# Fused token, attention and int8 layer: the split global term in one 128-row tile

## The reference

```
h   = einsum('bhid,oi,od->bho', x, weighted_sum, weight)      # x: 4 x 512 x 256 x 4
h   = concat(h, txt)                                          # 4 x (512 + 77) x 256
n   = layernorm(h)
hid = relu(n @ gate_w1 + b1);  gate = sigmoid(hid @ gate_w2 + b2)
U, V = n @ U_w, n @ V_w;       S = cumsum(V, axis=1)
glob = gate * U * S                                           # 32 numbers a row
h   = h + conv3(n) + glob @ out_w + out_b                     # out_w: 32 x 256
h   = h + int8_matmul(layernorm(h), rhs)
```

## Time and profile before

| | |
|---|---|
| median of 3 runs | 103.8 us (103.67 to 104.01) |
| profiled execution, first to last instruction | 102.7 us |
| busy: PE, DVE, ACT, POOL | 92.3, 82.5, 76.1, 70.1 us |
| mean granted clock of TensorE | 0.996 |
| chain that ended last: ACT, POOL, PE, DVE, DMA, issue | 23, 19, 16, 13, 11, 10% |

### The profile page before, as it was taken

One profiled execution on the slowest core, in us unless ns is written; L12 is line 12 of the kernel. 1 busy time (PEld: TensorE's weight loads), 2 busy tenths in 40 slices (PEclk: granted clock), 3 DMA queues, 4 the chain that ended last, 5 costly groups with the idle time before them and its releaser, 6 DMA issues.

```text
span 102.7 us, 2135 instructions
## 1 busy us (share of the span) xinstructions
PE 92.3 (90%) x686; PEld 83.8 (82%) x686; DVE 82.5 (80%) x224; ACT 76.1 (74%) x150; POOL 70.1 (68%) x133
## 2 busy tenths in 40 slices
PE   5999994999997999978989989999999788998870
PEld 5988894999696999968979969998897667987650
DVE  3377694489979988996999999899978988998731
ACT  1328646989996999938889987967698999927510
POOL 2000056979458709998997859998998959899940
PEclk9999999999999999999999999999999999999998
DMA  3999992679899999199993896788000230002513
GB/s 71 290 286 377 253 307 99 175 255 324 145 204 206 263 284 203 24 179 317 249 332 136 134 198 179 126 209 169 13 31 0 105 133 3 6 0 97 191 50 132
DMA packets 8137, 17.35 MB, mean 169 GB/s; under 512 B 855, under 2 KB 4799, under 8 KB 8127
## 3 DMA queue, kind: packets, MB, share of 16 engines
q0 software_dynamic: 2880, 10.49, 43.5%
q1 hardware_dynamic: 4815, 6.47, 19.9%
q10 hardware_dynamic: 432, 0.27, 0.9%
HBM read 14.81 MB, written 2.41 MB: 168 GB/s over the span
## 4 chain that ended last, share of the span: by engine, by line
ACT 23%; POOL 19%; PE 16%; DVE 13%; DMA 11%; issue 10%; SPq 4%; POOLq 0%; ACTq 0%
DMA x_sb<-x_dram 11%; POOL rstd L400 7%; ACT xn L619 4%; ACT x_low L523 4%; POOL rstd L399 4%; POOL x_high L425 4%; SPq L350 3%; DVE stats L694 3%; PE h_ps L1003 3%; ACT convT L573 2%; POOL shift L448 2%; ACT xc L629 2%; DVE amax L809 2%; ACT tmp L531 2%; ACT glob L603 2%
## 5 line engine op out<-in xcount | busy, mean ns | idle before, releaser
L908 PE MATMUL h_ps<-w_high,x_high 128*128 128x256 f32 x112 | 33.8, 302 | 0.1
L912 PE MATMUL h_ps<-w_high,x_low 128*128 128x256 f32 x112 | 31.3, 280 | 0.0
L910 PE MATMUL h_ps<-w_low,x_high 128*128 128x256 f32 x112 | 31.3, 279 | 0.0
L908 PEld LDWEIGHTS h_ps<-w_high,x_high 128*128 128x128 f32 x112 | 21.1, 188 | 1.0 <-issue 0.8
L910 PEld LDWEIGHTS h_ps<-w_low,x_high 128*128 128x128 f32 x112 | 21.1, 189 | 0.2
L912 PEld LDWEIGHTS h_ps<-w_high,x_low 128*128 128x128 f32 x112 | 21.1, 188 | 0.0
L399 POOL TENSOR_SCALAR rstd<-mv 128x2 f32<-128x2 f32 (+2 forms) x21 | 8.6, 410 | 17.4 <-DVE mv L697 16.7
L400 POOL TENSOR_TENSOR rstd<-rstd,exponent 128x2 f32<-128x2 f32 (+2 forms) x21 | 16.8, 798 | 1.8
L694 DVE BATCH_NORM_STATS2 stats<-h_ps 128x6 f32<-128x256 f32 (+1 forms) x36 | 13.8, 420 | 2.9 <-PE h_ps L912 1.6
L619 ACT ACTIVATE xn<-h_ps,shift,rstd 128x256 f32<-128x256 f32 x16 | 8.1, 559 | 6.3 <-POOL shift L448 6.3
L781 DVE SCALAR_TENSOR_TENSOR convT<-xnT,par_sb,convT 128x255 f32<-128x255 f32 (+1 forms) x24 | 12.2, 550 | 0.5 <-ACT convT L573 0.3
(11 more groups left out here) (109 smaller groups left out, 205.0 us busy)
## 6 DMA issues: line engine op xcount, KB each, us to landing
x_high<-x_dram POOLq DMA_DIRECT2D x10, 512.0 KB, 6.4
x_low<-x_dram POOLq DMA_DIRECT2D x10, 512.0 KB, 6.1
x_sb<-x_dram SPq DMA_DIRECT2D x4, 512.0 KB, 9.0
out_dram<-fin SPq DMA_DIRECT2D x8, 256.0 KB
x_sb<-x_dram SPq DMA_DIRECT2D x3, 256.0 KB, 4.3
par_sb<-par_dram SPq DMA_DIRECT2D x1, 325.0 KB, 8.4
txt_sb<-txt_dram SPq DMA_DIRECT2D x1, 308.0 KB
out_dram<-fin SPq DMA_DIRECT2D x4, 77.0 KB
```

The costliest lines, as they stand in the source:

```text
L908: nc.tensor.matmul(h_of(g)[:, t, :], x_high[:, g % RING, kc, at], w_high[:, kc, :], start=(kc == 0 and t == 0), stop=False, skip_group_che ...
L910: nc.tensor.matmul(h_of(g)[:, t, :], x_high[:, g % RING, kc, at], w_low[:, kc, :], start=False, stop=False, skip_group_check=True)
L912: last = nc.tensor.matmul(h_of(g)[:, t, :], x_low[:, g % RING, kc, at], w_high[:, kc, :], start=False, stop=(kc == KC - 1), skip_group_che ...
```

## The change

The tiles `glob3` and `outw3` go. A tile `parts` of 128 rows and 333 columns takes their place: rows 0 to 63 hold the high parts of `glob` as it lies (half 0, half 1), rows 64 to 127 the low parts. ACT makes the high parts of a batch in one copy of 64 rows by 333 columns, DVE the low parts in one subtraction of the same size. Both are at the place that the first half's had. The copy waits for both of POOL's multiplications, and `mix` for the whole batch's parts.

The output weights are laid out with zeros for each half: `out_w` is 128 rows by 2 x 256 columns, in which a half has the weights in its own two blocks of 32 rows (of the high and of the low parts) and zeros elsewhere. They are rounded once (`outw_high`, 128 x 512) and their low part is `outw_low` (128 x 512). `mix` is two products for a tile, `parts` by `outw_high` and `parts` by `outw_low`. (The term low by low, which was left out before, is now in the sum.) The parameters' DMA grows from 650 to 906 columns.

```diff
-    high=(24, 25, 46, 48, 69, 70, 89, 90),
-    low=(19, 20, 36, 38, 54, 57, 69, 72),
+    high=(-1, 24, -1, 46, -1, 69, -1, 89),
+    low=(-1, 19, -1, 36, -1, 54, -1, 69),
...
-    PAR = C_OUTW + D
+    PAR = C_OUTW + HALVES * D
...
-        glob3 = sb("glob3", [3 * R, 2, L], F32R)
-        outw3 = sb("outw3", [3 * R, D], F32R)
+        parts = sb("parts", [2 * HALVES * R, 2, PAIR + T], F32R)
+        outw_high = sb("outw_high", [P, HALVES, D], F32R)
+        outw_low = sb("outw_low", [P, HALVES, D], F32R)
...
-                for n in (0, 1):
-                    nc.scalar.activation(outw3[n * R:(n + 1) * R, :], outw, ACT.Copy).then_inc(outw_high, 1)
+                nc.scalar.activation(outw_high[:, :, :], outw, ACT.Copy).then_inc(outw_rounded, 1)
...
-                    b, half = divmod(g, HALVES)
-                    lo, hi = GLOB_RANGES[half]
-                    act.wait_ge(glob_ready, 2 * b + half + 1)
+                    b = g // HALVES
+                    act.wait_ge(glob_ready, 2 * (b + 1))
                     if b >= 2:
                         act.wait_ge(mix_done, ITEMS_PER_B * (b - 1))
-                    for n in (half, 2):
-                        nc.scalar.activation(glob3[n * R:(n + 1) * R, b % 2, lo:hi],
-                                             glob[half * R:(half + 1) * R, b % 2, 0:hi - lo],
-                                             ACT.Copy).then_inc(glob_high, 1)
+                    nc.scalar.activation(parts[0:HALVES * R, b % 2, :], glob[:, b % 2, :],
+                                         ACT.Copy).then_inc(glob_high, 1)
...
-                nc.vector.tensor_tensor(outw3[2 * R:3 * R, :], outw, outw3[0:R, :].bitcast(F32), ALU.subtract)
+                nc.vector.tensor_tensor(outw_low[:, :, :], outw, outw_high[:, :, :].bitcast(F32),
+                                        ALU.subtract).then_inc(outw_split, 1)
...
-                    dve.wait_ge(glob_high, 2 * g + 1)
-                    own, other = slice(half * R, (half + 1) * R), slice((1 - half) * R, (2 - half) * R)
-                    nc.vector.tensor_tensor(glob3[other, b % 2, lo:hi], glob[own, b % 2, 0:hi - lo],
-                                            glob3[own, b % 2, lo:hi].bitcast(F32), ALU.subtract).then_inc(glob_low, 1)
+                    dve.wait_ge(glob_high, b + 1)
+                    nc.vector.tensor_tensor(parts[HALVES * R:2 * HALVES * R, b % 2, :], glob[:, b % 2, :],
+                                            parts[0:HALVES * R, b % 2, :].bitcast(F32),
+                                            ALU.subtract).then_inc(glob_low, 1)
...
-                pe.wait_ge(glob_high, 2 * (HALVES * b + min(i + 1, HALVES)))
-                pe.wait_ge(glob_low, HALVES * b + min(i + 1, HALVES))
+                if j == 0:
+                    pe.wait_ge(outw_rounded, 1)
+                    pe.wait_ge(outw_split, 1)
+                pe.wait_ge(glob_high, b + 1)
+                pe.wait_ge(glob_low, b + 1)
+                half = min(i, HALVES - 1)
                 for t in range(nt):
-                    at = i * PAIR + t * P
-                    last = nc.tensor.matmul(h_item(j)[0:rows, t, :], glob3[:, b % 2, at:at + rows], outw3[:, :],
-                                            start=False, stop=True, skip_group_check=True)
+                    at = (i // HALVES) * PAIR + t * P
+                    nc.tensor.matmul(h_item(j)[0:rows, t, :], parts[:, b % 2, at:at + rows], outw_high[:, half, :],
+                                     start=False, stop=False, skip_group_check=True)
+                    last = nc.tensor.matmul(h_item(j)[0:rows, t, :], parts[:, b % 2, at:at + rows],
+                                            outw_low[:, half, :], start=False, stop=True, skip_group_check=True)
```

More of the change, by code:

```diff
@@ L130, in early_fusion_kernel @@
     RANGES = [(0, PAIR - 1), (PAIR - 1, L)]
-    GLOB_RANGES = [(0, PAIR), (PAIR, L)]
     with ExitStack() as ctx:
@@ L256, in early_fusion_kernel @@
         w2 = par_sb[:, C_W2:C_OUTW]
-        outw = par_sb[0:R, C_OUTW:PAR]
+        outw = par_sb[:, C_OUTW:PAR].rearrange("p (h d) -> p h d", h=HALVES)
         HID, URO, VRO = slice(0, GH), slice(GH, GH + R), slice(GH + R, P)
@@ L325, in early_fusion_kernel @@
         glob_low = sem("glob_low")
-        outw_high = sem("outw_high")
+        outw_rounded = sem("outw_rounded")
+        outw_split = sem("outw_split")
         diag_ready = sem("diag_ready")
@@ L405, in gated @@
                 if b >= 2:
-                    pool.wait_ge(glob_high, 2 * HALVES * (b - 1))
-                    pool.wait_ge(glob_low, HALVES * (b - 1))
+                    pool.wait_ge(glob_high, b - 1)
+                    pool.wait_ge(glob_low, b - 1)
                 pool.wait_ge(gate_ready, b + 1)
@@ L545, in txt_relu, with outw_round @@
                 nc.scalar.activation(hid_txt[:, :], uvg_ps[HID, 0:TB], ACT.Relu, bias=b1).then_inc(txt_hid, 1)
-            def outw_split():
+            def outw_round():
                 act.wait_ge(par_loaded, 16)
-                for n in (0, 1):
-                    nc.scalar.activation(outw3[n * R:(n + 1) * R, :], outw, ACT.Copy).then_inc(outw_high, 1)
+                nc.scalar.activation(outw_high[:, :, :], outw, ACT.Copy).then_inc(outw_rounded, 1)
             def txt_sigmoid():
@@ L646, in _ @@
                     txt_sigmoid()
-                    outw_split()
+                    outw_round()
                 for j in items(place, "put"):
@@ L735, in rhs_round, with outw_rest @@
                 last.then_inc(rhs_rounded, 1)
-            def outw_low():
-                dve.wait_ge(outw_high, 2)
-                nc.vector.tensor_tensor(outw3[2 * R:3 * R, :], outw, outw3[0:R, :].bitcast(F32), ALU.subtract)
+            def outw_rest():
+                dve.wait_ge(outw_rounded, 1)
+                nc.vector.tensor_tensor(outw_low[:, :, :], outw, outw_high[:, :, :].bitcast(F32),
+                                        ALU.subtract).then_inc(outw_split, 1)
             def txt_uv_out():
@@ L796, in _ @@
                 for g in groups(place, "low"):
[L797 to L800, removed]
-                    dve.wait_ge(glob_high, 2 * g + 1)
-                    own, other = slice(half * R, (half + 1) * R), slice((1 - half) * R, (2 - half) * R)
-                    nc.vector.tensor_tensor(glob3[other, b % 2, lo:hi], glob[own, b % 2, 0:hi - lo],
-                                            glob3[own, b % 2, lo:hi].bitcast(F32), ALU.subtract).then_inc(glob_low, 1)
+                    b = g // HALVES
+                    if b == 0:
+                        outw_rest()
+                    dve.wait_ge(glob_high, b + 1)
+                    nc.vector.tensor_tensor(parts[HALVES * R:2 * HALVES * R, b % 2, :], glob[:, b % 2, :],
+                                            parts[0:HALVES * R, b % 2, :].bitcast(F32),
+                                            ALU.subtract).then_inc(glob_low, 1)
                 for j in items(place, "scale"):
@@ L1120 @@
         gate_w2[half * GH:(half + 1) * GH, half * R:(half + 1) * R] = L0_attn_gate_w2
-    for a in (f(L0_attn_gate_b1)[:, None], np.tile(f(L0_attn_gate_b2), 2)[:, None], gate_w2, f(L0_attn_out_w)):
+    out_w = np.zeros((P, 2, D), x.dtype)
+    for half in range(2):
+        for first in (half * R, (2 + half) * R):
+            out_w[first:first + R, half] = L0_attn_out_w
+    out_w = out_w.reshape(P, 2 * D)
+    for a in (f(L0_attn_gate_b1)[:, None], np.tile(f(L0_attn_gate_b2), 2)[:, None], gate_w2, out_w):
         rows = np.zeros((P, a.shape[1]), a.dtype)
```

## The result

The changed kernel takes 105.06 us (median of 20 runs, 104.14 to 106.84) against 104.03 (20 runs, 103.17 to 104.89): a ratio of 1.0121, 95% interval 1.0095 to 1.0146, so 1.3 us slower. The medians of all runs differ by 1.0 us; the ratios leave out runs more than 1.5% above the fastest of the same kernel, among them 6 of the 12 of r7, 16 of the 35 of before that stand beside r9 to r12, and the profiled runs of r7 and r8. The forecast was 105.9 in a range from 104.4 to 106.9. The direction and the range held, the size of the loss was 1.3 instead of 2.1 us, and several terms behind it were wrong.

A forecast was written before the change was run, and what follows sets the result against it. No engine alone was taken to set the time, though PE has little left (busy 92.3 of 102.7 us). Lateness grew 0.19, 0.43, 0.67, 0.88, 1.29, 2.13 us; 103.8 + 2.1 = 105.9 us, range 104.4 to 106.9.

The forecast's parts named there:

- The wait for both multiplications in batch 3: Batch 3: the copy waits for POOL's second multiplication, so the first mix begins at 86.87 instead of 86.63, 0.24 us later.
- the sign that the prediction named (0.7): Sign of being right: PE waits 0.7 us for DVE's low part in front of batch 3's first mix.
- The same wait in batch 2: Batch 2: the copy waits for both multiplications, so the mix begins at 72.15 instead of 71.74, 0.40 us later.
- D = 0.19 at the gates of batch 0: Start: lateness against before (D), 0.45 us for 131 KB more parameters less 0.26 for the weights' single copy.
- POOL's load, forecast at 17.6: Sign of being right: POOL's load for group 3 starts at about 17.6 us; before it started at 17.15.
- D = 0.43: Batch 0: lateness when the first mix begins, at 37.3 instead of about 36.9, behind DVE's later subtractions.
- the waits that the prediction named as signs: PE waiting for DVE's low part before the first mix of batches 0, 2 and 3: 0.2, 0.4 and 0.7 us.
- ACT gets gaps in place of the copies: All batches: ACT's 5.5 us of removed work was to become idle time, with no gain counted in the forecast time.
- The rival that ended on the other side: "Faster", chance 0.10: ACT's list paces 50 to 60 and 85 to 90 us; removed copies give 102.0 or about 102.8.
- The walk: Method: follow lateness D from PE wait to PE wait, batches 0 to 3; added work disappears in some waits; total 2.13 us.
- D grows: Batch 3: 0.24 us for the later first mix and 0.60 for three items' added products, taking D from 1.29 to 2.13.
- the sum, 2.13: Whole kernel: final lateness D after batch 3, 2.13 us, added to 103.8 to give 105.9 us.

The follow-up runs named there:

- r7: Changed kernel without the addition in memory of group 7 (its low part is minus the high part): ratio 1.0013 to the kernel before.
- r9: Kernel before without the addition in memory of group 7 (its low part is minus the high part): ratio 0.9985 to the kernel before.
- r12: Changed kernel with group 7's negations and second addition moved earlier, and copy and subtraction split to set the text's columns apart: ratio 1.0031 to the kernel before.
- r8: Kernel before with each mix product done twice, 20 more products and nothing else changed: ratio 1.0088 to the kernel before, 0.9 us.
- r2: Changed kernel with the output weights in a DMA of their own behind x of group 2: ratio 1.0140 to the kernel before.
- r3: Changed kernel without its second mix product (the weights' low part left out), so 20 products as before: ratio 0.9935 to the kernel before.
- r10: Changed kernel with group 7's negations and second addition moved a little earlier, behind POOL's scale of group 5: ratio 1.0071 to the kernel before.
- r5: Changed kernel with the last batch alone done the old way (four copies, two subtractions, one product a tile): ratio 1.0121 to the kernel before.
- r6: Changed kernel with group 7's negations and additions moved further ahead, into ACT's gaps at 55 and 59 us: ratio 1.0121 to the kernel before.
- r1: The changed kernel again, unchanged, as yardstick on the chip of the three runs after it: ratio 1.0124 to the kernel before.

## Why the prediction was right in sign and wrong in its parts

**Right, with its size.** Durations: 482 and 502 ns for the new copy and subtraction, 0.12 us for one more product, 2.4 us of them in all (PE's busy time, which counts overlap, rose by 1.6). The wait for both multiplications in batch 3 was forecast at 0.24 us: the gates of batch 3 to its first mix took 3.37 us before and 3.63 after. POOL, DVE and PE in that place, the answer to the earlier trace rows:

```profile
85.44 0.31 POOL L417 TENSOR_TENSOR glob<-gate_txt,us_txt 64x77 f32<-64x77 f32 x1
```

```profile
86.30 0.50 DVE L799 TENSOR_TENSOR parts<-glob,parts 64x333 fp32r<-64x333 f32 x1 [0.60 <-ACT parts L601]
```

```profile
86.95 0.36 PE L1013 MATMUL h_ps<-outw_high,parts 128*128 128x256 f32 x1 [0.70 <-DVE parts L799]
```

The 0.70 us that PE stands in front of this mix is the sign that the prediction named (0.7). The same wait in batch 2 was forecast at 0.40 and shows at 0.4 in r7, once the DMA is out of its way.

**Wrong: the start.** "D = 0.19 at the gates of batch 0" came from 131 KB at 290 GB/s. r2 took all the weights out of the way and gained nothing that can be told, and POOL's load, forecast at 17.6, began at 16.58. No run shows this term. The step that failed is to price a transfer by its bytes where the wait behind it was not shown to be one for bandwidth, against a start that differs by over 1 us between profiles.

**Wrong: the first mix.** "With 0.05 for the signal it now begins at 37.3, D = 0.43." In the trace DVE's subtractions end at 36.32 and PE mixes at 36.47, right behind its convolution and without a wait, the answer to the earlier trace rows:

```profile
35.11 0.68 DVE L736 TENSOR_TENSOR outw_low<-par_sb,outw_high 128x512 fp32r<-128x512 f32 x1
35.82 0.50 DVE L799 TENSOR_TENSOR parts<-glob,parts 64x333 fp32r<-64x333 f32 x1
```

```profile
36.47 0.36 PE L1013 MATMUL h_ps<-outw_high,parts 128*128 128x256 f32 x1
```

DVE was not late here: its parts were ready 0.15 us before PE came. Of the waits that the prediction named as signs, 0.2, 0.4 and 0.7 us in batches 0, 2 and 3, only the last stands in the changed kernel.

**Wrong: "ACT gets gaps in place of the copies".** This put the relief at nothing. r3 has the relief and not the products: 0.7 us faster. The rival that ended on the other side had this mechanism right, and it decides once the products are away; with them it lost. The table gives the relief 0.8 us from transpose 1 to 3 and 0.4 from 3 to 6. Of the first, 0.67 us is one instruction of POOL (below), which took 0.80 us in r3's profile as in the changed kernel's and 1.47 before. So how much of the 0.7 us belongs to ACT's and DVE's freed time is open.

**Missing: the arrival of group 7's low part.** This is the step that matters. The walk went from PE's wait to PE's wait as they stood in the trace of before, and that list held no DMA. But the transfer was there, just in time. Before, its two halves landed at 68.7 and 72.9 us (5.5 and 7.4 behind their issue at 63.19 and 65.55), and the first products that need them began at 68.80 and 73.05, the second some 0.3 later than PE's spacing of 0.12 would have had it (PE, timeline of before):

```profile
68.80 0.43 PE L908 MATMUL h_ps<-w_high,x_high 128*128 128x256 f32 x1
...
72.64 0.28 PE L912 MATMUL h_ps<-w_high,x_low 128*128 128x256 f32 x1
73.05 0.36 PE L908 MATMUL h_ps<-w_high,x_high 128*128 128x256 f32 x1
```

In the changed kernel PE was ahead by 0.9 us at 52 us. ACT's negation stood behind a relu that waits for PE, so the additions were issued only 0.7 and 1.1 us earlier; they took 6.2 and 8.7 us and landed at 68.7 and 73.1, no earlier. PE ran into them for 1.3 us. That engines ran ahead is not all of it: in r8, where nothing is relieved, they took 6.0 and 8.2 us, and PE waited for both. r7 and r9 together put about 1.0 of the 1.3 us of slowdown on this arrival, give or take 0.6 or more; by the means of all runs, none left out, it would be 0.4 (they also free POOL of two issues, in both kernels alike). r10 and r12 win part of it back by moving only the issue, r12 with the text's columns apart as well. Why the additions took longer than before is not settled; both halves were in flight at once, and no run measured that alone.

**Wrong by size: the tail.** "D grows" by 0.84 in batch 3. The products cost 0.46 between the mixes, as forecast, and the 0.24 wait came (0.26 in the trace). But 0.15 was won ahead of the transpose of group 7, and 0.23 behind the last mix, the fifth added product included. There a small DVE instruction had run beside POOL's addition before and taken 0.24 longer, and no longer does. 0.34 is left in the trace, too little for r5's timed ratio.

So the sum, 2.13, held two terms that no run shows (0.19 and 0.24), lacked a gain (the relief) and a loss (the arrival), and came within 0.9 us of the result because these go against each other. That the range held is in part luck: the last mix began at 92.70, 0.8 later than before and not 2.1, and 0.4 to 1.0 us of the loss came from a wait that the walk did not have.

## What to carry to other kernels

Split a trade of one engine's work for another's in two runs, relief alone and load alone: here they were 0.7 us faster and 2.0 slower (0.9 in the kernel that is not relieved), and no single trace shows that. Before walking from wait to wait, look for transfers that landed just in time (here 0.1 us before their first use); they are missing from the list of waits because they were in time, and here they did not move with the engines. A gap that opens can be filled, but only behind what the path goes through: the same transfer moved too far ahead (r6) delayed POOL's scale of group 5 and gained nothing.

## What the runs showed of the hardware

One instruction of POOL took 0.67 us longer in some profiles than in others. POOL's power on two numbers a row took 0.71 to 0.73 us in most places. In the kernel before one of them took 1.47, with a DVE product of two inputs that began 0.15 us behind it (POOL, then DVE):

```profile
39.90 1.47 POOL L400 TENSOR_TENSOR rstd<-rstd,exponent 128x2 f32<-128x2 f32 x1
```

```profile
40.05 0.42 DVE L759 TENSOR_TENSOR x_sb<-qrhs,rs_row 128x256 f32<-128x256 bf16 x1
```

In the changed kernel the same pair, at the same distance, took 0.80:

```profile
39.73 0.80 POOL L401 TENSOR_TENSOR rstd<-rstd,exponent 128x2 f32<-128x2 f32 x1
```

```profile
39.88 0.42 DVE L757 TENSOR_TENSOR x_sb<-qrhs,rs_row 128x256 f32<-128x256 bf16 x1
```

It was 1.47 in all four profiles of the old layout and in three (r2, r5, r7) of the ten of the new, and PE's transpose of group 3 came 20.17 to 20.49 us behind that of group 1 in these, 19.34 to 19.71 in the others. What it costs at the end is not shown: the profiled runs of r2 and r5, with it, took 105.4 and 105.0 us, those of the changed kernel and r1, without it, 105.05 and 105.15. What decides between the two is not settled, and that the DVE product is the cause is read from its place alone. The Trainium skill ("GPSIMD Engine Reference", the SBUF interfaces row of its specifications) states that POOL's port is shared with DVE and disturbed by instructions with two SBUF inputs. The pair in the trace fits that, 1.47 us against 0.80, and shows in addition that it can go either way at the same distance.

The reverse may exist too: DVE's small L811 took 0.41 us in the kernel before while POOL's addition (L480) was ending, and 0.17 in the changed one, where it came behind it:

```profile
94.25 0.41 DVE L811 TENSOR_SCALAR nstep<-amax 128x2 f32<-128x2 f32 x1
```

```profile
95.03 0.17 DVE L808 TENSOR_SCALAR nstep<-amax 128x2 f32<-128x2 f32 x1
```
